# Spreading the closing rows to all partitions: DMA copies in place of products with a picking matrix

## What is computed

```python
x = x + tanh(g_xattn[0]) * xattn(layernorm(x), ctx_512, Wq, w_kc_q, w_kc_kv, W_qr, W_kr, Wo)   # 16 heads, 256 keys of 64
x = x + tanh(g_ffn[0]) * ffn(layernorm(x), ...)

def ffn(x, ...):
    x_norm = layer_norm(x, in_gamma, in_beta)
    thought = x_norm[:, -1, :] @ agg_w + agg_b          # one row per batch: 4 x 256
    for _ in range(4):
        t = layer_norm(thought, pn_gamma, pn_beta)
        t = gelu(t @ d1_w + d1_b)
        thought = thought + (t @ d2_w + d2_b)
    broadcast = (thought @ bc_w + bc_b)[:, None, :]     # one row per batch, for all 256 rows of it
    gate = sigmoid(x @ gate_w + gate_b)
    return layer_norm(x + gate * broadcast, out_gamma, out_beta)
```

## Time and profile before

| | |
|---|---|
| median of 3 runs | 229.07 us (228.8 to 229.17) |
| profiled execution | 227.19 us |
| its span in the profile | 225.4 us |
| PE busy | 199.4 us, 88% |
| DVE busy | 171.3 us, 76% |
| ACT busy | 104.0 us, 46% |
| POOL busy | 75.4 us, 33% |
| DMA | 18.14 MB, mean 81 GB/s |

### The profile page before, as it was taken

One profiled execution on the slowest core, in us unless ns is written; L12 is line 12 of the kernel. 1 busy time (PEld: TensorE's weight loads), 2 busy tenths in 40 slices (PEclk: granted clock), 3 DMA queues, 4 the chain that ended last, 5 costly groups with the idle time before them and its releaser, 6 DMA issues.

```text
span 225.4 us, 6424 instructions
## 1 busy us (share of the span) xinstructions
PE 199.4 (88%) x2607; PEld 172.3 (76%) x2607; DVE 171.3 (76%) x406; ACT 104.0 (46%) x189; POOL 75.4 (33%) x155
## 2 busy tenths in 40 slices
PE   0999997999969998998999998998999999997740
PEld 0878975878859896996898887797897898786620
DVE  3265698989966899897985598687646688999964
ACT  2456756368233664217646255644443426533120
POOL 7930110005989479874100200001000122353423
PEclk9999999999999999999999999999999999999955
DMA  7999996236170640000300400000302100100101
GB/s 163 250 291 303 267 278 171 70 125 157 42 201 0 189 95 3 3 0 8 91 6 0 99 0 3 3 0 6 96 4 46 52 0 4 46 21 19 37 23 47
DMA packets 21877, 18.14 MB, mean 81 GB/s; under 512 B 5556, under 2 KB 19924, under 8 KB 21848
## 3 DMA queue, kind: packets, MB, share of 16 engines
q1 hardware_dynamic: 21848, 17.74, 30.1%
HBM read 12.16 MB, written 1.05 MB: 59 GB/s over the span
## 4 chain that ended last, share of the span: by engine, by line
PE 44%; DVE 27%; SPq 9%; issue 7%; DMA 5%; ACT 3%; POOL 3%; POOLq 0%; DVEq 0%; ACTq 0%
PE ps L1044 8%; PE ps L1012 5%; DVE row_max L750 4%; PE ps L1031 4%; DMA kv_hi<-kv_hi 4%; PE ps L882 4%; PE ps L1033 4%; PE ps L884 3%; PE ps L883 3%; DVE bn L668 2%; PE ps L1131 2%; DVE q_split L744 2%; DVE q_split L742 2%; PE ps L1056 2%; DMA q_hi<-shift 2%
## 5 line engine op out<-in xcount | busy, mean ns | idle before, releaser
L631 ACT ACTIVATE probs<-ps 128x512 f32<-128x512 f32 x64 | 35.8, 595 | 27.4 <-PE ps L1033 25.7
L750 DVE TENSOR_REDUCE row_max<-ps 128x2 f32<-128x512 f32 x64 | 42.3, 682 | 5.4 <-PE ps L1012 4.8
L539 POOL TENSOR_SCALAR var_eps<-mean_var 128x1 f32<-128x1 f32 (+1 forms) x29 | 7.0, 241 | 112.9 <-DVE mean_var L669 112.5
L1044 PE MATMUL ps<-kv,probs 128*64 128x65 f32 x1024 | 34.3, 223 | 0.0
L1044 PEld LDWEIGHTS ps<-kv,probs 128*64 128x64 f32 x1024 | 31.7, 137 | 2.9 <-issue 2.0
L1031 PE MATMUL ps<-q_hi,kv_lo 128*128 128x512 f32 x64 | 27.2, 426 | 2.1 <-DMA q_hi<-shift 1.9
L1012 PE MATMUL ps<-kv_hi,q_split 128*128 128x256 f32 x128 | 25.9, 301 | 2.6 <-DVE q_split L744 1.4
L1033 PE MATMUL ps<-q_split,kv_hi 128*128 128x512 f32 x64 | 25.3, 395 | 0.0
L1012 PEld LDWEIGHTS ps<-kv_hi,q_split 128*128 128x128 f32 x128 | 19.7, 188 | 6.8 <-issue 3.3
L882 PE MATMUL ps<-xT_lo,A_hi 128*128 128x256 f32 x64 | 18.7, 293 | 0.1
L617 ACT ACTIVATE q_split<-ps 64x512 fp32r<-64x512 f32 x16 | 9.5, 591 | 19.8 <-PE ps L884 19.8
(11 more groups left out here) (139 smaller groups left out, 438.9 us busy)
## 6 DMA issues: line engine op xcount, KB each, us to landing
q_hi<-q_split SPq DMA_DIRECT2D x16, 256.0 KB, 3.7
wq<-in_L_xattn_Wq SPq DMA_DIRECT2D x4, 512.0 KB, 9.1
wo<-in_L_xattn_Wo SPq DMA_DIRECT2D x2, 1024.0 KB, 11.0
w_rest<-in_L_ffn_d_w SPq DMA_DIRECT2D x2, 1024.0 KB, 5.5
wkcq<-in_L_xattn_w_kc_q SPq DMA_DIRECT2D x8, 192.0 KB, 5.4
out_x<-fin SPq DMA_DIRECT2D x8, 128.0 KB
wqr<-in_L_xattn_W_qr SPq DMA_DIRECT2D x4, 192.0 KB, 5.7
x<-in_x SPq DMA_DIRECT2D x8, 64.0 KB, 5.8
```

The lines of the kernel that those rows point to most:

```text
L631: act.activation(probs[:, n % PROBS_BUFS, lb, :], bank(e), ACT.Exp).then_inc(free[place[e]], 1)
L750: dve.reduce_max(row_max[:, s % 2, 2 * j:2 * j + 2], bank(e).rearrange("p (h l) -> p h l", h=2), AX.X).then_inc(free[place[e]], 1)
L1044: ins = pe.matmul(bank(e)[q:q + 64, hh * (DC + 1):(hh + 1) * (DC + 1)], probs[:, n % PROBS_BUFS, lb, hh * P + q:hh * P + q + 64], kv1[:, k ...
```

## The change

The products and the picking matrix go: `row_pick`, its load on SP (L468), its input, the PE part of `bc_rows` with its two waits, ACT's copies, and `bc_rows` as a member of the PSUM ring. In their place SP, at the same three places of the plan, issues DMA copies whose source is one row of `bc4`, read again for each partition to be written. Step 0 waits for `bc4` and copies four slabs of 32 partitions (slot 4 of `bc_all`), each counting up `bc_slab_in`; steps 1 and 2 copy two whole-batch rows each to 128 partitions, counting up `bc_rows_in`. DVE waits for the slabs in `f_pre(0)` and for the rows in `f_pre(4)` (`NB` is 4, `QB` 32, `P` 128, `D` 256).

```diff
@@ RINGS
-                  "up", "down", "downT", "bc", "bc_rows"),
+                  "up", "down", "downT", "bc"),
@@ block.sync
-                    sp.dma_start(row_pick[:, :, :], t["row_pick"]).then_inc(row_pick_in, 16)
...
+                if e[0] == "bc_rows":
+
+                    if e[1] == 0:
+                        taken(sp, ("bc", 0))
+                    for b in range(NB) if e[1] == 0 else range(2 * e[1] - 2, 2 * e[1]):
+                        rows = slice(QB * b, QB * (b + 1)) if e[1] == 0 else slice(0, P)
+                        n = rows.stop - rows.start
+                        sp.dma_start(bc_all[rows, NB if e[1] == 0 else b, :],
+                                     bc4[b:b + 1, :].unsqueeze(1).to_broadcast([1, n, D])
+                                     ).then_inc(bc_slab_in if e[1] == 0 else bc_rows_in, 16)
@@ block.scalar
-                if name == "bc_rows":
-                    filled(act, e)
-                    bs = slice(2 * e[1], min(2 * e[1] + 2, NB + 1))
-                    act.activation(bc_all[:, bs, :].rearrange("p b d -> p (b d)"), bank(e)[:, 0:D * (bs.stop - bs.start)],
-                                   ACT.Copy).then_inc(free[place[e]], 1)
@@ block.vector, f_pre
-                        for i in range(3):
-                            taken(dve, ("bc_rows", i))
+                        dve.wait_ge(bc_slab_in, 16 * NB)
+                    if u == NB:
+                        dve.wait_ge(bc_rows_in, 16 * NB)
@@ block.tensor
-                if name == "bc_rows":
-
-                    taken(pe, ("bc", 0))
-                    pe.wait_ge(row_pick_in, 16)
-                    for i in range(2 if e[1] < 2 else 1):
-                        ins = pe.matmul(bank(e)[:, i * D:(i + 1) * D], row_pick[:, 2 * e[1] + i, :], bc4[:, :],
-                                        start=True, stop=True)
-                    ins.then_inc(done, 1)
```

More of the change, by code:

```diff
@@ L287, in gated_cross_attention_ffn @@
         fin_in = sb("fin_in", [P, 2, D])
-        row_pick = sb("row_pick", [NB, NB + 1, P])
         w_rest = sb("w_rest", [P, KB * HID])
@@ L296, in gated_cross_attention_ffn @@
         hi_done = sem("hi_done")
-        ident_in, rope_in, ctx_in, row_pick_in = sem("ident_in"), sem("rope_in"), sem("ctx_in"), sem("row_pick_in")
+        ident_in, rope_in, ctx_in, bc_rows_in = sem("ident_in"), sem("rope_in"), sem("ctx_in"), sem("bc_rows_in")
         x_in = [sem(f"x_in{i}") for i in range(3)]
@@ L315, in gated_cross_attention_ffn @@
         kv_made = sem("kv_made")
+        bc_slab_in = sem("bc_slab_in")
         ones_row = sem("ones_row")
@@ L1170, in shape_constants @@
     consts = np.concatenate([np.eye(P, dtype=f), by_partition(cos), by_partition(sin)], axis=1)
-    row_pick = np.repeat(np.eye(NB, dtype=f)[:, :, None], P, axis=2)
-    row_pick = np.concatenate([row_pick, np.repeat(np.eye(NB, dtype=f), QB, axis=1)[:, None, :]], axis=1)
-    return {"consts": np.ascontiguousarray(consts), "row_pick": np.ascontiguousarray(row_pick)}
+    return {"consts": np.ascontiguousarray(consts)}
 def kernel(**inputs):
```

## The result

The changed kernel takes 238.47 us (median of 6 runs, 236.59 to 240.24), the kernel before 228.94 us. The ratio of the fast runs is 1.0446, with a 95% interval of 1.039 to 1.050; the medians keep the slow ones (over 1.5% above the fastest, here one of six) and alone would give 1.042. The change costs about ten microseconds. The profiled execution has a span of 235.4 us and a time of 237.32 us.

The account below looks back on a forecast made before the run. No engine bounds the whole; the chain is PE's from 173.13 to 179.87 and DVE's from 183. DVE's start 8.7 us later, the 1.8 gain swallowed, plus 1.3 for the clock: +10.0 on 229.07, so 239.1 us; range 226.6 to 245.

Parts of the forecast that it names:

- the case to which it gave 0.64: Copies from 173 at 20 to 30 GB/s with `q_hi_load(7)` queued behind them; time 235 to 245 us, chance 0.64.
- The gain, 1.8 us: PE chain from 173.13: without ten passes (2.44 us), what follows comes 1.6 to 2.0 us earlier, taken as 1.8.
- The removed load of `row_pick`: On SP at 47.55, 0.36 us ahead of `q_hi_load(1)`; its removal was said to be worth nothing.
- the ring's turns: PSUM ring loses three turns of `bc_rows`; entries behind wait for `bc` and `shiftT(6)`, free by 172, so nothing lost.
- The rate, 25 GB/s, 26.2 us: Eight copies from 173.3 read single partitions at 25 GB/s; 655,360 bytes take 26.2 us, the slabs 5.2 of them.
- The skill's figure: For the copies' reads: 27.6 GB/s from partitions 0 to 3 would make them 23.7 us, the time 2.5 us less.
- The slabs in time, the rows in time: Slabs done 179.2 ahead of `f_pre(0)` at 181.25; rows signalled 200.2 against `f_pre(4)` at 200.7: both hidden.
- `q_hi_load(7)` behind the copies, landed at 202.4: Queued behind the copies, it lands at 202.4 with unit 7's shift row; PE stands at `st(7,0,0)` from 190.65.
- From `st` to DVE, 2.4 + 1.3 us: From `st(7,0,0)` to DVE's start on `ctxT(6,0)`: 2.4 us as today, plus 1.3 for TensorE at half clock.
- The work moves as a block: From DVE's start on `ctxT(6,0)`, 8.7 us later, to the end the work is DVE's and shifts as a whole.
- the clock's cost: TensorE at half clock after some twelve idle us, near 202: from 0 to some 4 us, taken as 1.3.
- The threshold: No stall at `st(7,0,0)` if loads land by 191.8: copies done by 188.9, 655 KB in 15.6 us, 42 GB/s.

Follow-up runs that it names:

- second probe: Kernel before plus six waited-for SBUF copies at its end: four 256 KB pairings of partition halves, two from one partition; pairings 187 GB/s, landed in 2.8 to 2.9 us.

## Why the prediction was right

It had 239.1 us; measured were 238.47. Its range, 226.6 to 245, held a gain as well as a loss, so that the number falls into it says little; the case to which it gave 0.64, a slow read with `q_hi_load(7)` behind it, is the one that came. By its steps:

- **The gain, 1.8 us.** Right: 1.9 at `f_pre(0)`, 1.8 at `st(7,0,0)` in the kernel without any spreading, 2.1 at its end. The removed load of `row_pick`, ACT's copies and the ring's turns were not taken out singly; with the products they come to these 1.8.
- **The rate, 25 GB/s, 26.2 us.** Right in size: 27 GB/s, 24 us, the first packets near 173.2 and the rate up at 197.4. **The reason given for it was wrong.** The prediction read the two q_hi copies (181 and 331 GB/s) as a limit on partitions that reads and writes share, and took the per-engine rate from there. The second probe moved 187 GB/s for every pairing, shared or not.
- **The skill's figure.** The Trainium skill (SBUF — State Buffer, section "Door 1: The DMA port swizzle (why `[64,N]` ≈ `[32,N]`)") gives 27.6 GB/s for partitions 0 to 3. The traces agree: 27 GB/s from these four rows one after the other, and 26 from partition 0. Its figure of near 200 GB/s for 64 partitions, which the prediction set aside over the 331, agrees with the second probe's 187 and not with that copy.
- **The slabs in time, the rows in time.** Right: `f_pre(0)` didn't wait, and no other use of `bc_all` did.
- **`q_hi_load(7)` behind the copies, landed at 202.4.** PE went on at 201.67. Two details were off. The prediction had `q_hi_load(7)` issued at 177.2 and left to the queue what followed; SP was held instead, and issued it at 185.29. The load that landed last was the shift row, by 0.2 us. And it named the order of one queue as the mechanism; the shift row sent from ACT's queue landed just as late, so it is not the queue alone. Moving one load, or the copies, to another queue did not help. A load can still pass by being issued first: `q_hi_load(7)` did, in 3.5 us.
- **From `st` to DVE, 2.4 + 1.3 us.** 3.56 measured, of which 1.1 the clock's.
- **"The work moves as a block" to the end.** Here the size was off: DVE's step came 9.2 us late (205.23 against 196.06), the end 10.0. The prediction took the clock's cost as over at DVE's step; with PE kept busy it was 1.7 us to the end. Of the 0.8 us that the tail is longer than before (30.2 against 29.3 from DVE's step) the clock has about 0.5; the rest stays open. The two errors, DVE's step 0.9 us earlier than the 206.1 forecast and the tail 0.8 us longer, cancel, so the closeness of 239.1 is partly luck.
- **The threshold.** The prediction put it at 42 GB/s for 640 KB, a landing by 191.8. 384 KB at 27 GB/s take as long as 640 KB at 45, where by the prediction the gain of 1.8 us should have been whole; PE waited 1.9 us and the kernel came out equal to before. So the point lies higher than it was put. The terms missing are two: the shift row, said to land with the q_hi copies, landed 1.4 us behind them (190.30 against 188.9), and the clock fell.

## What to carry to other kernels

A broadcast by DMA from one row in SBUF ran at 27 GB/s here, though the engines were 0.83 busy with it: divide the bytes written by that, and ask what else has to land within that time. Sending the rows to HBM first held SP for 1.5 us, landing included, and each copy of 128 KB then landed some thirteen microseconds sooner; here that turned a loss of 4.5% into a gain of 1.3 to 1.7%. A slow copy isn't harmful by its own deadline only: the small load behind it, in either queue that was tried, was what ended last. Whether rows on partitions far apart, in place of 0 to 3, would be read faster together was not tried.

## What was not expected of the hardware

- SP issues six copies at 0.59 us each and is then held for 4.55 to 4.78 us at each further one, close to the 4.9 us that 128 KB take at 27 GB/s. A slow copy so takes the issuing engine too, and every wait and issue in its order. POOL wasn't held: it issued all eight within 4.42 us.
- An 8 KB load from ACT's queue took 14.3 us behind slow copies on SP's queue, where it takes 1.8 to 2.1 on free engines.
- With 256 KB between 64 and 64 partitions, four different pairings moved alike (187 GB/s each in windows of 1.4 us), while two copies of this size issued back to back had 181 and 331 GB/s.
- The granted clock fell 1.2 us behind a stall of 1.90 us, while PE worked: the eight transposes took 1.77 us, where they take 1.04 at 1.00. Behind the 1.90 us stall near 66 in the kernel before it did not fall.
